# Taking the first of four layer-norm statistics three steps later on VectorE in a batched attention pipeline

## The chip, the cores and the metric

The kernel runs on one core of one Trainium2 chip. The metric is the device time of one execution in microseconds (us); lower is better.

## The reference, cut to what matters

There are 8 batches of 512 tokens with 256 features. Each batch goes through an attention layer whose keys are picked by an argmax, and then all tokens go through a layer of 8 experts of which each token takes 2.

```python
x = x + tanh(g_xattn) * xattn(layernorm(x), ctx)
x = x + tanh(g_ffn) * ffn(layernorm(x))

def xattn(q, kv):                       # per batch; 16 heads of 16
    qp = q @ Wq.T
    scores = qp @ kv.T                  # 512 x 512
    idx = argmax(scores)                # one key row per query
    mk, mv = split(kv[idx] @ Wkv.T)
    attn = softmax(heads(qp) @ mk.T / 4)
    return (attn @ mv) @ Wc.T

def ffn(x):                             # 8 experts, top 2
    top_v, top_i = top_k(x @ gate_w, 2)
    ...                                 # gelu(x @ w1[e] + b1[e]) @ w2[e] + b2[e], weighted
```

Many queries choose the same key, so the kernel keeps each chosen key once, with a count, in at most 192 slots. The softmax then runs over 192 slots and not over 512 keys.

## The kernel before, in words

The program has two large parts. `flow` does everything up to the queues of tokens for the experts; `experts` then runs 39 tiles of 256 tokens through their experts. The change is in `flow`.

`flow` is a software pipeline written out by hand. A generator, `each_step`, goes over periods `p` from -4 to 9 and over 32 steps in each. Every one of the five engines walks through the same (period, step) pairs, and at each step issues the pieces of work that a table of step numbers gives it. An engine carries out its pieces strictly in that order, and waits on semaphores for what other engines or DMAs have yet to deliver. In period `p` these batches are in work:

- batch `p + 4`: its `x` is loaded by SP (step 15, `load_x`, into the single buffer `x_in`), VectorE (DVE) takes one `bn_stats` for each of its four tiles of 128 tokens (`x_stats`, L876, steps in `DVE_X_STATS`) and joins them (`x_moments_of`, step 24). GpSimd (POOL) turns the variance into a factor (L584, step 26) and normalises the four tiles (L592, steps 26 to 29).
- batch `p + 3`: TensorE (PE) transposes the normalised `x` (L1022, step 14) and projects it to queries (L1039, steps 16 and 17).
- batch `p + 2`: PE makes the scores (L1064, steps 5, 7, 9, 11, one tile of queries each), DVE finds each maximum and its index (L808, L809), POOL marks the chosen key (L559). PE counts how often each key is chosen (L1074, step 15); DVE turns that into used or unused (L821, L823, step 17); PE ranks the used keys (L1082, L1083, step 18); DVE makes their positions in the 192 slots (`positions`, step 19, L828 to L838). For batch 0 DVE also writes the 0/1 matrix `place` itself (L836); for the other batches POOL does (L579, step 20). PE then packs keys and values into slots (L1090, L1095, step 22), and ScalarE (ACT) copies them to `k_st` and `v_st` (L673 to L676, step 23).
- batch `p + 1`: PE makes the logits again in query-major form to find each row's maximum (`logits_b`, L1107, one tile a step from step 25 of the period before), and DVE reduces each tile (`take_max`, L849). These tiles and the scores go through a ring of PSUM banks: four banks in negative periods, two from period 0 on. So PE can be at most that many tiles ahead of DVE.
- batch `p`: the softmax and the weighted sum. Batch `p - 1`: output projection, second layer norm, gate and queues.

Periods -4 to -1 fill the pipeline. Within a step, DVE's code comes in this order (much is left out): heads, keys and values, best key, `add`, `x_stats`, `x1_stats`, `used_keys` (17), `positions` (19), `shift_of` (20), `x_moments_of` (24), and last `take_max`. `x_stats` waits for the transfer of `x`:

```python
            def x_stats(b, t):
                dve.wait_ge(x_loaded, 16 * (b + 1))
                chain.step(v.bn_stats(stats[:, 0, t, :], x_in[:, t, :]))
```

and `positions` begins with a wait for the ranks and for all earlier steps of DVE's own chain:

```python
                dve.wait_ge(ranks_ready, s + 1)
                chain.settle()
```

Next to this, 32 pieces of expert weights of 512 KB each are loaded by SP into two staging buffers (L444, L447), rounded by ACT (L770), and their remainder is formed by POOL (L635). SP issues its transfers in program order too.

Of the kernel before, what the change touches and what calls it, by code (L numbers as in the profile page):

```python
# [181 lines left out]
def program(nc, x, ctx_t, g, wq_t, wkv_t, wc_t, gate_w, w1, b1_t, w2, b2, out):  # L182
# [11 lines left out]
    with ExitStack() as whole:  # L194
# [36 lines left out]
        k.dve_steps, k.pool_steps = sem("dve_steps"), sem("pool_steps")  # L231

        flow(nc, k, sem, sb, ps)

        general = Programs(), Programs()
# [5 lines left out]
def flow(nc, k, sem, sb, ps):  # L241
# [6 lines left out]
    with ExitStack() as own:  # L248
# [116 lines left out]

        DVE_HEADS = 13
        DVE_BEST, DVE_KV, DVE_USED, DVE_PLACE = (6, 8, 10, 12), 9, 17, 19
        DVE_X_STATS, DVE_X_MOMENTS = (18, 22, 22, 23), 24
        DVE_ADD, DVE_STATS, DVE_MOMENTS, DVE_SHIFT = (11, 14), (15, 15, 16, 16), 17, 20
        DVE_SPLIT_MAX, DVE_COPY_MAX, DVE_CHOOSE, DVE_SHARES, DVE_QUEUE = 25, 27, 29, 31, 0  # L370

# [2077 lines left out]
```

## Time and profile before

| | |
|---|---|
| median of 3 runs | 993.09 us (992.86 to 994.03) |
| span of the profiled execution (first to last instruction) | 992.7 us |
| filling of the pipeline, periods -4 to -1 | about the first 100 us |
| `flow` up to the end | about 537 us |
| `experts` | the rest, about 456 us |
| TensorE busy | 832.3 us (84%) |
| VectorE busy | 517.9 us (52%) |
| mean granted TensorE clock | 0.914 of full speed |

The profile is of one execution. It gives no time of its own beside its span; the span is 0.4 us under the median of the runs. Busy shares are means over stages with different limits, so each stage has to be read by itself: which engine waits, and for whom. In a timeline, a row is a group of like instructions that follow each other on one engine, with the start, the time from the first start to the last end, and in brackets how long the engine had been idle before it and what ended that.

### The profile page before, as it was taken

Reading aid. Unit: us, or ns where it says so; the run is one execution under the profiler, and the core shown is the slowest. Engines: PE = TensorE matmul, PEld = TensorE weight load, DVE = VectorE, ACT = ScalarE, POOL = GpSimd, SP = SyncE. Lnnn points to the kernel's source line nnn. Section 1 sums busy time; section 2 is a strip of 40 time slices with the busy share of each in tenths; the row PEclk is TensorE's granted clock in tenths of the full one; section 3 lists DMA queues with packets and bytes.
Section 4 is the critical chain, followed back from the end, with each engine's and each line's share of the span. In section 5 each row is a group of like instructions: output and inputs, shape, how many; then the busy total and the mean of one; then the engine's idle time right before and its main releaser. Section 6 shows DMA issues by size and latency. Waiting matters only on the chain. (4 is left out here: it accounts for less than half of the span.)

```text
span 992.7 us, 20863 instructions
## 1 busy us (share of the span) xinstructions
PE 832.3 (84%) x6508; PEld 579.8 (58%) x6509; DVE 517.9 (52%) x1534; ACT 376.7 (38%) x770; POOL 438.1 (44%) x475
## 2 busy tenths in 40 slices
PE   3675899899898989887610899999999999999994
PEld 1243345344343534433310699899989989988984
DVE  3475567766766677762330345444544454454451
ACT  1312263636363544666320333333333433333330
POOL 4766463666566545436541033333433343333334
PEclk9867899989997989898755799999999999999998
DMA  4653424433445261244224122221332233223210
GB/s 160 147 108 107 75 66 90 129 82 108 97 128 98 64 136 49 82 134 138 77 74 165 56 44 46 48 45 33 56 48 41 43 58 48 43 47 49 44 14 1
DMA packets 65691, 76.40 MB, mean 77 GB/s; under 512 B 7392, under 2 KB 59360, under 8 KB 65504
## 3 DMA queue, kind: packets, MB, share of 16 engines
q1 hardware_dynamic: 51328, 58.74, 22.7%
q0 software_dynamic: 14304, 16.93, 9.6%
q8 instruction: 30, 0.49, 0.2%
q14 instruction: 29, 0.24, 0.1%
HBM read 47.68 MB, written 29.53 MB: 78 GB/s over the span
## 5 line engine op out<-in xcount | busy, mean ns | idle before, releaser
L2389 PE MATMUL ps_h<-x_hi,w_split 128*128 128x256 bf16 x1248 | 212.7, 274 | 0.0
L2403 PE MATMUL ps_y<-w_split,hidden 128*128 x1248 | 206.4, 273 | 0.0
L698 ACT ACTIVATE prob<-ps_a 128x512 f32<-128x512 f32 x192 | 113.0, 603 | 181.5 <-PE ps_a L1127 108.2
L2389 PE MATMUL ps_h<-x_lo,w_split 128*128 128x256 bf16 x624 | 171.0, 274 | 0.0
L2403 PE MATMUL ps_y<-w_split,h_lo 128*128 x624 | 170.1, 273 | 0.0
L2299 ACT ACTIVATE hidden<-ps_h,bias 128x256 f32<-128x256 f32 x312 | 131.1, 471 | 88.6 <-PE ps_h L2389 88.6
L849 DVE TENSOR_REDUCE row_max<-ps_d 128x2 f32<-128x384 f32 x237 | 127.9, 551 | 60.8 <-PE ps_d L1107 59.2
L2273 POOL DMA_INDIRECT out<-y,token_at x78 | 131.0, 1680 | 43.8 <-POOL token_at L2271 30.3
L2389 PEld LDWEIGHTS ps_h<-x_hi,w_split 128*128 x1248 | 122.8, 98 | 14.5
L2403 PEld LDWEIGHTS ps_y<-w_split,hidden 128*128 128x128 bf16 x1248 | 122.1, 98 | 14.1
L2269 POOL TENSOR_TENSOR token_f<-tails,ones_f 128x2 f32<-128x2 f32 x39 | 7.8, 200 | 267.5 <-DVE y L2345 266.3
L2342 DVE TENSOR_TENSOR y<-ps_y,b_all 128x512 f32<-128x512 f32 x39 | 27.0, 692 | 174.5 <-PE ps_y L2403 174.5
L1107 PE MATMUL ps_d<-k_st,w_split 96*128 96x192 bf16 x474 | 84.5, 268 | 25.7 <-DVE row_max L849 19.2
L2356 DVE TENSOR_TENSOR h_lo<-hidden 128x512 bf16<-128x512 f32 x156 | 99.7, 686 | 11.3 <-ACT hidden L2299 10.3
L2288 ACT CAST x_hi<-ps_x 128x512 bf16<-128x512 f32 x39 | 22.9, 586 | 213.5 <-PE ps_x L2376 213.5
L635 POOL TENSOR_TENSOR w_split<-w_stage,w_split 128x1024 bf16<-128x1024 f32 x32 | 68.0, 2132 | 63.8 <-ACT w_split L770 63.8
L1107 PEld LDWEIGHTS ps_d<-k_st,w_split 96*128 96x128 bf16 x474 | 40.0, 103 | 77.6 <-DVE row_max L849 32.0
L1144 PE MATMUL ps_o<-prob,v_st 128*32 128x512 f32 x512 | 77.1, 678 | 3.0 <-ACT prob L698 3.0
L611 POOL DMA_INDIRECT queue<-rows,slot x64 | 62.9, 982 | 19.4 <-issue 17.1
L2389 PEld LDWEIGHTS ps_h<-x_lo,w_split 128*128 x624 | 61.4, 98 | 7.4
L2403 PEld LDWEIGHTS ps_y<-w_split,h_lo 128*128 128x128 bf16 x624 | 61.1, 98 | 7.1
L1064 PE MATMUL ps_d<-ctx_sb,q_t 128*128 128x512 f32 x112 | 57.8, 640 | 2.2 <-DVE row_max L849 1.4
(206 smaller groups left out, 1070.8 us busy)
## 6 DMA issues: line engine op xcount, KB each, us to landing
w_stage<-w SPq DMA_DIRECT2D x32, 512.0 KB, 4.1
xg<-queue SPq DMA_DIRECT2D x39, 260.0 KB, 2.8
w_split<-q_split SPq DMA_DIRECT2D x24, 256.0 KB, 7.9
x_in<-x SPq DMA_DIRECT2D x8, 512.0 KB, 3.8
ctx_sb<-ctx_t SPq DMA_DIRECT2D x8, 512.0 KB, 3.6
x<-x SPq DMA_DIRECT2D x8, 512.0 KB, 3.8
q_split<-q_hl SPq DMA_DIRECT2D x16, 256.0 KB, 3.5
out<-x SPq DMA_DIRECT2D x8, 512.0 KB, 5.0
```

Source lines behind the costliest of these rows:

```text
L611: pool.indirect_dma_start(k.queue[:], bass.IndirectOffsetOnAxis(ap=slot[:, t, c:c + 1], axis=0), rows[:, t, :], None).then_inc(scattered, 16)
L635: g.tensor_tensor(lo, stage, hi, ALU.subtract).then_inc(w_lo, 1)
L698: a.activation(prob[n % 2][:, j, :], ps_a[i % 2][:], ACT.Exp, scale=SCALE).then_inc(exp_ready, 1)
L849: v.tensor_reduce(row_max[:, t, 2 * pair:2 * pair + 2], bank[:, 0:2 * SLOTS].rearrange("p (h r) -> p h r", h=2), AX.X, ALU.max).then_inc(m ...
L1064: last = t_.matmul(ps_da[n][:], q_t[:, kt, t * P:(t + 1) * P], ctx_sb[:, kt, :], start=(kt == 0), stop=(kt == KT - 1))
L1107: last = t_.matmul(ps_da[n][:, c * SLOTS:(c + 1) * SLOTS], q_st[m % 3][0:ROW_MAX, 2 * pair + c, t * P:(t + 1) * P], k_st[0:ROW_MAX, m % 3, ...
L1144: last = t_.matmul(ps_o[j * VW:(j + 1) * VW, :], values, probs, start=(key_tile == 0), stop=(key_tile == SLOT_TILES - 1))
L2273: pool.indirect_dma_start(k.out_rows, bass.IndirectOffsetOnAxis(ap=token_at[:, t:t + 1], axis=0), y[s][:, t, :], None, bounds_check=B * L ...
L2299: last = a.activation(hidden[s][:, f, :], ps_h[n][:, c, :], ACT.Gelu, bias=bias[s][:, f:f + 1])
L2356: v.tensor_tensor(h_lo[s][:, both, :], hidden[s][:, both, :], h_hi[s][:, both, :], ALU.subtract).then_inc(h_lo_ready, 1)
L2389: last = t_.matmul(ps_h[n][:, c, :], k.w1_split[:, bass.ds(e, 1), part, kt, f].rearrange("p a f -> p (a f)"), xs[s][:, kt, :], start=(q == ...
L2403: last = t_.matmul(ps_y[s][:, t, :], hs[s][:, f, token], k.w2_split[:, bass.ds(e, 1), part, f, :].rearrange("p a d -> p (a d)"), start=(q ...
```

## The change

One number in a table moves from 18 to 21: the step at which VectorE takes the first of the four `bn_stats` of batch `p + 4`. The other three stay at steps 22, 22 and 23. Nothing is added or removed, and no buffer, transfer or semaphore changes.

```diff
         DVE_HEADS = 13
         DVE_BEST, DVE_KV, DVE_USED, DVE_PLACE = (6, 8, 10, 12), 9, 17, 19
-        DVE_X_STATS, DVE_X_MOMENTS = (18, 22, 22, 23), 24
+        DVE_X_STATS, DVE_X_MOMENTS = (21, 22, 22, 23), 24
         DVE_ADD, DVE_STATS, DVE_MOMENTS, DVE_SHIFT = (11, 14), (15, 15, 16, 16), 17, 20
```

The order of instructions on PE, ACT, POOL and SP is the same before and after. On DVE it differs in six of the eight batches' `x` (2 to 7). The first place is period -2, where no `take_max` work exists yet. These are VectorE's instructions there before; `used`, `unused`, `position` and `chosen` (here the 0/1 matrix of places) belong to batch 0, `stats<-x_in` to batch 2:

```order
L821 TENSOR_SCALAR used<-count 128x4
L823 TENSOR_SCALAR unused<-used 128x4
L878 BN_STATS stats<-x_in 128x6
L828 TENSOR_TENSOR position<-ps_r,unused 128x4
L829 COPY total<-ps_r 128x4
L831 SCALAR_TENSOR_TENSOR offset<-ones_f,total 128x4
L832 TENSOR_TENSOR position<-position,offset 128x4
L836 TENSOR_SCALAR chosen<-column,position 128x192 x4
L838 COPY n_chosen<-offset 128x1
L878 BN_STATS stats<-x_in 128x6 x3
L885 BN_AGGR moments<-stats 128x2 x4
L849 TENSOR_REDUCE row_max<-ps_d 128x2 x2
```

And these are VectorE's instructions at the same place of the changed kernel:

```order
L821 TENSOR_SCALAR used<-count 128x4
L823 TENSOR_SCALAR unused<-used 128x4
L828 TENSOR_TENSOR position<-ps_r,unused 128x4
L829 COPY total<-ps_r 128x4
L831 SCALAR_TENSOR_TENSOR offset<-ones_f,total 128x4
L832 TENSOR_TENSOR position<-position,offset 128x4
L836 TENSOR_SCALAR chosen<-column,position 128x192 x4
L838 COPY n_chosen<-offset 128x1
L878 BN_STATS stats<-x_in 128x6 x4
L885 BN_AGGR moments<-stats 128x2 x4
```

The first statistic, and with it the wait for the transfer of `x`, has gone from ahead of the positions and places to behind them.

The second place stands for the full pipeline (periods 0 to 3). This is the difference on VectorE there, with `row_max` the reduction of one tile of `logits_b`:

```order
 L821 TENSOR_SCALAR used<-count 128x4
 L823 TENSOR_SCALAR unused<-used 128x4
-L849 TENSOR_REDUCE row_max<-ps_d 128x2
-L878 BN_STATS stats<-x_in 128x6
-L849 TENSOR_REDUCE row_max<-ps_d 128x2
+L849 TENSOR_REDUCE row_max<-ps_d 128x2 x2
 L828 TENSOR_TENSOR position<-ps_r,unused 128x4
 L829 COPY total<-ps_r 128x4
```

```order
 L870 RECIPROCAL inverse<-ps_r 128x16
 L871 TENSOR_TENSOR heads<-ps_r,inverse 128x4x4x16
+L878 BN_STATS stats<-x_in 128x6
 L849 TENSOR_REDUCE row_max<-ps_d 128x2
 L878 BN_STATS stats<-x_in 128x6 x2
```

Here the statistic moves from between two reductions, ahead of the positions, to behind the heads of a group, ahead of the reduction of step 21.

## Rows read from the trace of the kernel before

**Rows 1.** The page: busy times by engine, and the last chain by line.
```profile
PE 832.3 (84%) x6508; PEld 579.8 (58%) x6509; DVE 517.9 (52%) x1534; ACT 376.7 (38%) x770; POOL 438.1 (44%) x475
...
PE ps_h L2389 21%; PE ps_y L2403 20%; PE ps_x L2376 2%; DMA xg<-queue 1%; DMA out<-y,token_at 0%; POOL out L2273 0%; DVE y L2342 0%; DVE x_lo L2334 0%; ACT x_hi L2288 0%; DVEq L2230 0%; SPq L2201 0%; SPq L2244 0%; SPq L2240 0%; DVE y L2345 0%; POOL token_f L2269 0%
```

**Rows 2.** Waits from 43 to 56 us: total, times, longest.
```profile
DVE stats L878 <- DMA x_in<-x: 11.0, 1, 11.0
...
PE ps_e L1090 <- DVE chosen L836: 9.5, 1, 9.5
...
POOL variance L584 <- DVE moments L885: 4.7, 1, 4.7
```

**Rows 3.** Timeline of VectorE, period -2: start, us, what, count.
```profile
39.69 0.17 DVE L823 TENSOR_SCALAR unused<-used 128x4 f32<-128x4 bf16 x1
50.84 0.43 DVE L878 BATCH_NORM_STATS2 stats<-x_in 128x6 f32<-128x256 f32 x1 [10.98 <-DMA x_in<-x]
...
51.84 0.16 DVE L832 TENSOR_TENSOR position<-position,offset 128x4 f32<-128x4 f32 x1
52.04 0.81 DVE L836 TENSOR_SCALAR chosen<-column,position 128x192 bf16<-128x192 f16 x4
...
52.83 1.07 DVE L878 BATCH_NORM_STATS2 stats<-x_in 128x6 f32<-128x256 f32 x3
54.00 0.38 DVE L885 BATCH_NORM_AGGREGATE moments<-stats 128x2 f32<-128x6 f32 x4
56.23 1.02 DVE L849 TENSOR_REDUCE row_max<-ps_d 128x2 f32<-128x384 f32 x2 [1.85 <-PE ps_d L1107]
```

**Rows 4.** Timeline of TensorE, periods -2 and -1.
```profile
43.21 0.17 PE L1083 MATMUL ps_r<-used,ones_bf 128*128 128x4 bf16 x1
52.90 0.87 PE L1090 MATMUL ps_e<-chosen,key_cols 128*98 128x192 bf16 x4 [9.53 <-DVE chosen L836]
53.57 1.18 PE L1095 MATMUL ps_e<-value_cols,chosen 128*128 128x17 bf16 x24
55.71 0.80 PE L1107 MATMUL ps_d<-k_st,w_split 96*128 96x192 bf16 x4 [0.95 <-issue]
...
61.11 3.75 PE L1064 MATMUL ps_d<-ctx_sb,q_t 128*128 128x512 f32 x4
...
65.86 1.91 PE L1064 MATMUL ps_d<-ctx_sb,q_t 128*128 128x512 f32 x4
```

**Rows 5.** Timeline of ScalarE, period -2.
```profile
45.37 1.04 ACT L667 CAST q_hl<-q_t 128x1024 bf16<-128x1024 f32 x1
54.79 0.51 ACT L673 ACTIVATE k_st<-ps_e,key_add,key_mul 98x192 bf16<-98x192 f32 x1 [8.38 <-PE ps_e L1095]
```

**Rows 6.** Timeline of SP's DMA issues: the load of batch 2's x.
```profile
42.33 0.50 SPq L452 DMA_DIRECT2D x_in<-x  x1
```

**Rows 7.** Timeline of GpSimd, period -1.
```profile
62.82 2.12 POOL L635 TENSOR_TENSOR w_split<-w_stage,w_split 128x1024 bf16<-128x1024 f32 x1
66.47 0.19 POOL L558 CAST best<-top_at 128x1 f32<-128x1 uint32 x1 [1.53 <-DVE top_at L809]
...
69.38 0.19 POOL L558 CAST best<-top_at 128x1 f32<-128x1 uint32 x1 [1.03 <-DVE top_at L809]
```

**Rows 8.** Timeline of VectorE in period 0, around steps 18 and 23.
```profile
130.03 0.42 DVE L878 BATCH_NORM_STATS2 stats<-x_in 128x6 f32<-128x256 f32 x1
132.85 0.56 DVE L849 TENSOR_REDUCE row_max<-ps_d 128x2 f32<-128x384 f32 x1 [2.40 <-PE ps_d L1107]
...
138.61 0.56 DVE L849 TENSOR_REDUCE row_max<-ps_d 128x2 f32<-128x384 f32 x1 [0.86 <-PE ps_d L1107]
```

**Rows 9.** Windows: length, busy us (count) of PE, PEld, DVE, ACT, POOL; PEclk, DMA share, GB/s.
```profile
56.00:61.00 5.00, 5.00 (x26) 2.05 (x23) 4.78 (x11) 1.62 (x2) 5.00 (x4) 0.50 0.00 0
61.00:65.00 4.00, 3.95 (x7) 1.48 (x6) 1.46 (x4) 0.00 (x0) 3.94 (x3) 0.50 0.91 209
65.50:68.00 2.50, 2.50 (x23) 1.25 (x12) 1.98 (x6) 1.21 (x2) 1.42 (x2) 1.00 1.14 116
```

## The prediction

> **What bounds the kernel now.** I read the page first. TensorE is busy 84% of the span and the last chain holds only lines of the expert part [rows 1], so that part is bound by TensorE matmuls in a fixed order and the change can't touch it; it will start earlier or later by what `flow` gains or loses. The chain ends there and says nothing on `flow`, so I went through the waits, stage by stage, around every place where the order of VectorE changes. In the full pipeline these waits are a few tenths of a microsecond. In period -2 they are large: VectorE waits 11.0 us for the transfer of batch 2's `x`, and in the same stretch TensorE waits 9.5 us for VectorE's places of batch 0 [rows 2]. The timelines show that these are one wait. VectorE is done with `unused` at 39.86, then stands until 50.84 in front of the first `bn_stats`, and only behind it come positions and places, done at 52.85 [rows 3]. TensorE had the ranks ready at 43.38, packs from 52.90, and starts `logits_b` at 55.71 [rows 4]. So the reader should see a queue: positions need nothing but the ranks, yet they stand behind an instruction that needs a DMA issued only at 42.33 [rows 6].
>
> **The change at period -2.** It takes the waiting instruction out of the way of the positions. Step by step:
>
> *Places.* From the end of the first statistic (50.84 + 0.43 = 51.27) to the end of the places (52.04 + 0.81 = 52.85) it is 1.58 us [rows 3]. They can start when the ranks are there, 43.38: places at 43.38 + 1.6 = 45.0.
>
> *Pack.* 52.90 to 53.57 + 1.18 = 54.75 is 1.85 us [rows 4]: done at 46.85. ACT's copy of the packed keys stands behind the rounding of the queries, which ends at 45.37 + 1.04 = 46.41 [rows 5], so it is free. From its start (54.79) to the first `logits_b` (55.71) it is 0.92 us [rows 4, 5]: `logits_b` starts near 47.8, 7.9 us earlier.
>
> *What is late next.* VectorE must reduce those tiles, and its reductions stand behind all four statistics of batch 2. Nothing in the chain of that transfer is moved: SP issues it at 42.33 as before [rows 6], so I keep the landing at 50.84. Four statistics take 0.43 + 1.07 = 1.5 us, the gap to the moments is 54.00 - 53.90 = 0.1, the moments take 0.38 [rows 3]: the first `row_max` can start at 50.84 + 2.0 = 52.8. By then TensorE has filled the four banks. Before, it started at 56.23, and it had waited 1.85 us for TensorE [rows 3]. The gain here is 56.23 - 52.8 = 3.4 us. The other 4.5 us of TensorE's head start are lost to the transfer, which still bounds the stage.
>
> *Does the shift live on?* From 56.23 to the scores of batch 1 at 61.11 VectorE is busy 4.78 of 5 us [rows 9], with TensorE held by the bank ring, so the scores start when the reductions free a bank: they move with VectorE, to about 57.7. Two engines move by less. The moments end at 52.8 in place of 54.38, so POOL's variance comes only 1.6 us earlier; before, it waited 4.7 us for them [rows 2, 3]. POOL's last piece before the chosen keys ends at 64.94, then at 63.3; the first index, which it awaited for 1.53 us until 66.47, comes at 63.1. That costs 0.2 us at that one instruction, and the next has a wait of 1.03 us to take it back [rows 7]. SP's next weight piece hangs on the same POOL work and also moves by 1.6 us only, and so the query loads behind it; these are needed a period later. So I let the full 3.4 us pass into period -1 and from there on, since every later piece hangs on a semaphore and not on a fixed time.
>
> **The change in period -1 and in the full pipeline.** The four statistics cost the same; one moves. In period 0 the first one stood at 130.03, and the reduction behind it then waited 2.40 us for TensorE until 132.85 [rows 8]. It was hidden in that idle time, so the positions behind the reduction gain nothing. At its new place it comes between busy instructions and delays the reductions of steps 21 and 22 and the last statistic by 0.42 us. The next reduction, at 138.61, has waited 0.86 us for TensorE [rows 8]: it takes the delay in, and 0.44 us stay. TensorE's ring of two banks needs the reduction of step 21 only at step 23. Four periods have this pattern; price 0, and if that cover were gone 4 x 0.42 = 1.7 us. The nearest row gives cover, so I take 0.
>
> **The clock.** TensorE's granted clock is 0.50 (1.2 GHz) from 56 to 65 us although TensorE is busy 5.00 of 5 us with bf16 `logits_b` from 56 to 61; it is 1.00 (2.4 GHz) from 65.5, after some 4 us of float32 scores. The first tile of scores takes 3.75 us at the low level, a later one 1.91 at the high one [rows 4, 9]. I take the rise at the same instruction as before, so the price of the clock is 0, between -1.84 (the first tile of scores is already fast) and +1.84 for each further tile that stays slow.
>
> The Trainium skill, "TensorE: Matmul & The Clock Gate", Part 1, says that the idle state is the throttled one and that sustained matmul activity releases it. By that rule the earlier pack and `logits_b` would make the clock rise before the first scores, and the sum would be 1.84 us lower. The trace does not agree in that stretch: 5 us of unbroken `logits_b` did not raise it.
>
> **The sum.** -3.4 + 0 + 0 = -3.4 us. From the span 992.7 that is 989.3; the median lies 0.4 above the span, so 989.7 us, 0.34% less.
>
> **The rivals.**
>
> 1. *The clock rises sooner.* TensorE works from about 45 to 49 and again from 52.8, and no longer lies idle for 9.5 us in one piece. If that lifts the clock before the first scores, -3.4 - 1.84: 987.8 us. For it: two bursts and less idle time. Against it: rows 9, where dense `logits_b` did not do it.
>
> 2. *Part of the gain is absorbed.* Either the side that moves by 1.6 us (POOL, SP, the query loads) turns out to be last somewhere in period -1, or the 0.42 us show in each of four full periods. Both leave some 1.7 us: 991.4 us. Against it: POOL's wait of 1.53 us, and the 0.86 us of cover in VectorE [rows 7, 8].
>
> 3. *Nothing comes of it.* The transfer of `x` still holds batch 2, and a later wait in the filling of the pipeline (another transfer, the weights) ends when it did: 993.1 us. For it: the 7.9 us on TensorE shrink to 3.4 at once. Against it: all loads are issued in reply to work that moves too.
>
> 4. *Slower: the clock stays low for longer.* The place is the four tiles of scores in period -1, with `logits_b` now paced by VectorE and more often idle before them. If all four ran at 1.2 GHz, the price is 4 x 1.84 = 7.4, less the 3.4 gained: +4.0, 997.1 us. From the third slow tile on (5.5 - 3.4 = +2.1) it decides. Against it: float32 scores raised the clock before within the first tile.
>
> **How the numbers follow.** Two tenths of a percent is 2.0 us, about what a measurement of this kernel can tell from no change. Chances: my forecast 0.68 (own range 989.0 to 990.4), rival 1 0.09, rival 2 0.13, rival 3 0.06, rival 4 0.04. Faster takes the forecast, rival 1 and the better edge of rival 2: 0.79. The rest of rival 2 and rival 3 are no change: 0.17. Slower 0.04. The range reaches from rival 1 to rival 2, 987.8 to 991.4, with about half of each beyond it or at its edge.
>
> **What the profile would show.** Right: VectorE's places end near 45.0 and its wait for the transfer of `x`, until about 50.8, follows them; the pack starts near 45.0; `logits_b` starts near 47.8; the first `row_max` near 52.8; the first scores of batch 1 near 57.7, still 3.75 us long; from then on every row of period 0 stands 3.4 us earlier, with an idle time of some 2.8 us ahead of the reduction of step 18 and of some 0.4 us ahead of that of step 23. Wrong: the transfer landing later than 50.84 moves the gain down one for one; a wait of TensorE longer than before in period -1 for the chosen keys or the places, written by POOL, is rival 2; scores at another length are rivals 1 or 4.

## The result and the profile after

The changed kernel took 988.11 us (median of 5 runs, 986.64 to 988.61) against 992.86 us before on the same chip (991.54 to 994.03). The ratio is 0.9946 with a 95% interval of 0.9930 to 0.9963: 5.4 us less, or 3.7 to 7.0 us. (The two medians by themselves lie 4.75 us apart; the interval belongs to the ratio.) The span of the profiled execution went from 992.7 to 986.8 us. The forecast was 3.4 us less. Its sign and its place were right; its size lies just below that interval.

VectorE in period -2 after the change, the rows that answer to [rows 3] (timeline: start, us, what, count, idle before):

```profile
42.59 0.16 DVE L828 TENSOR_TENSOR position<-ps_r,unused 128x4 f32<-128x4 f32 x1 [4.78 <-PE ps_r L1083]
...
43.26 0.81 DVE L836 TENSOR_SCALAR chosen<-column,position 128x192 bf16<-128x192 f16 x4
...
47.54 1.41 DVE L878 BATCH_NORM_STATS2 stats<-x_in 128x6 f32<-128x256 f32 x4 [3.41 <-DMA x_in<-x]
49.05 0.38 DVE L885 BATCH_NORM_AGGREGATE moments<-stats 128x2 f32<-128x6 f32 x4
49.34 0.99 DVE L849 TENSOR_REDUCE row_max<-ps_d 128x2 f32<-128x384 f32 x2
```

The positions now wait only for the ranks (4.78 us, until 42.54), the places end at 44.07, and the wait for `x` stands behind them. The first reduction starts 1.80 us behind the landing of `x` (49.34 - 47.54). Before, it was 5.39 us (56.23 - 50.84, [rows 3]).

TensorE at the same place, the rows that answer to [rows 4]:

```profile
44.12 0.53 PE L1090 MATMUL ps_e<-chosen,key_cols 128*98 128x192 bf16 x4 [1.58 <-DVE chosen L836]
...
46.43 0.80 PE L1107 MATMUL ps_d<-k_st,w_split 96*128 96x192 bf16 x4 [0.95 <-issue]
47.02 0.85 PE L1107 MATMUL ps_a<-k_st,w_split 96*128 96x192 bf16 x4
49.93 0.97 PE L1107 MATMUL ps_d<-k_st,w_split 96*128 96x192 bf16 x4 [2.06 <-DVE row_max L849]
...
54.19 3.75 PE L1064 MATMUL ps_d<-ctx_sb,q_t 128*128 128x512 f32 x4
```

The 9.53 us of idle time ahead of the pack are 1.58 us. TensorE fills four banks (two rows of four matmuls, two to a tile), then stands for 2.06 us until VectorE has reduced one. The first scores come at 54.19, 6.92 us earlier than at 61.11, and still take 3.75 us.

What differs beside that is upstream of the change. SP's issue of the same `x`, the row that answers to [rows 6]:

```profile
40.35 0.50 SPq L452 DMA_DIRECT2D x_in<-x  x1
```

It is 1.98 us earlier than in the profile before, and the landing is 3.30 us earlier (47.54 against 50.84), so the transfer also took 1.3 us less. Yet no instruction ahead of that point has changed its place. The difference in the first reduction splits without rest: 56.23 - 49.34 = 6.89 = 3.30 (landing) + 3.59 (5.39 - 1.80, what lies between landing and reduction). Whether the 3.30 are chance or belong to the change was the open question.

Period 0, the rows that answer to [rows 8]:

```profile
126.31 0.56 DVE L849 TENSOR_REDUCE row_max<-ps_d 128x2 f32<-128x384 f32 x1 [2.74 <-PE ps_d L1107]
...
129.20 0.43 DVE L878 BATCH_NORM_STATS2 stats<-x_in 128x6 f32<-128x256 f32 x1
...
132.07 0.56 DVE L849 TENSOR_REDUCE row_max<-ps_d 128x2 f32<-128x384 f32 x1 [0.53 <-PE ps_d L1107]
```

The statistic left an idle time that grew from 2.40 to 2.74 us, and took 0.33 of the 0.86 us of cover ahead of the reduction of step 23. Both reductions stand 6.54 us earlier than before: nothing is gained or lost between them.

### The profile page after: what moved, and what is told of

Same layout as the page of the kernel before. It is cut to its first block and busy times, and to the rows that moved or that the text cites. A ratio compares the mean times of both kernels' runs of the same rounds, so it can differ in the third digit from the quotient of the medians.

```text
span 986.8 us, 20863 instructions
## 1 busy us (share of the span) xinstructions
PE 834.3 (85%) x6508; PEld 580.4 (59%) x6509; DVE 518.1 (53%) x1534; ACT 376.8 (38%) x770; POOL 438.5 (44%) x475
## 5 line engine op out<-in xcount | busy, mean ns | idle before, releaser
L635 POOL TENSOR_TENSOR w_split<-w_stage,w_split 128x1024 bf16<-128x1024 f32 x32 | 68.1, 2134 | 64.6 <-ACT w_split L770 64.5
```

Of the source, the lines that this page charges most:

```text
L635: g.tensor_tensor(lo, stage, hi, ALU.subtract).then_inc(w_lo, 1)
```

## The experiments

Theory A: the change takes the 3.6 us between the landing of `x` and the first reduction, and the landing itself moves by chance. Its rivals were B (the earlier landing comes from the change), C (the other five places give a part), D (something else bounds the filling of the pipeline) and later E and F. All ratios are to runs of the kernel before on the same chip, each with a 95% interval.

### The kernel before once more, and the changed kernel once more

No edit.

> The kernel before once more, to see how far two profiles and two sets of times of one program lie apart. Theory A (the change is worth the 3.6 us that lie between the landing of x and the first reduction in the two profiles, 5.39 against 1.80 us, and the other 3.3 us between the two profiles are chance: an earlier landing of the first transfers and of x): ratio 1.000 within 0.1%, and in its profile a landing of x that differs from 50.84 us by one us or more, with the first reduction again 5.4 us behind it. Theory B (the landing of x is earlier because of the change): a landing of x at 50.8 within 0.5 us here.

Measured: ratio 0.9998 (0.9985 to 1.0010), span 990.4 us. In its profile `x` landed at 47.23 us, not at 50.84:

```profile
47.23 0.43 DVE L878 BATCH_NORM_STATS2 stats<-x_in 128x6 f32<-128x256 f32 x1 [9.12 <-DMA x_in<-x]
...
48.02 0.87 DVE L831 TENSOR_TENSOR_SCAN offset<-ones_f,total 128x4 f32<-128x4 f32 x1
...
53.31 1.02 DVE L849 TENSOR_REDUCE row_max<-ps_d 128x2 f32<-128x384 f32 x2 [1.85 <-PE ps_d L1107]
```

So the unchanged program lands `x` 3.6 us apart in two executions, earlier even than the changed one did. The reduction is 6.08 us behind the landing; 0.7 of that is the scan at L831, which took 0.87 in place of 0.17 us (more on that in the last section).

> The changed kernel once more. Theory A: the first reduction again 1.8 to 2.0 us behind the landing of x, the landing itself somewhere between 47 and 51 us; faster by 3.6 us, a ratio of 0.9964. Theory B: landing near 47.5 us again and a ratio near 0.9946, 5.4 us.

Measured: 0.9953 (0.9936 to 0.9969), span 987.2 us. This time `x` landed at 49.92 us, and the reduction again followed 1.80 us behind:

```profile
49.92 1.40 DVE L878 BATCH_NORM_STATS2 stats<-x_in 128x6 f32<-128x256 f32 x4 [7.28 <-DMA x_in<-x]
51.43 0.38 DVE L885 BATCH_NORM_AGGREGATE moments<-stats 128x2 f32<-128x6 f32 x4
51.72 0.99 DVE L849 TENSOR_REDUCE row_max<-ps_d 128x2 f32<-128x384 f32 x2
```

In the four profiles of the old order with no transfer moved (before, once more, all but batch 2, third time) `x` landed at 49.4 us in the mean, in the four of the changed order at 49.2. The single early landing was chance, and theory B falls. The ratio, 4.7 us, lies between the two expectations and its interval holds both.

### Only batch 2, and all but batch 2

```diff
-                for t in due(p + 4, DVE_X_STATS, step):
+                for t in due(p + 4, (21, 22, 22, 23) if p == -2 else DVE_X_STATS, step):
```

This is on the kernel before; the other one has `(18, 22, 22, 23) if p == -2` on the changed kernel.

> Only batch 2's first statistic (period -2) is taken at step 21; all others stay at step 18. Theory A: all of the gain is there, so this is as fast as the changed kernel, within 0.1%. Rival C (a part of the gain comes from the five other places, each worth up to 0.42 us): 1 to 2 us slower than the changed kernel.

> Batch 2's first statistic stays at step 18, ahead of the positions; all others go to step 21. Theory A: no change to the kernel before, within 0.1%, with VectorE again waiting for x ahead of the positions. Rival C: 1 to 2 us faster than before.

Measured: only batch 2, 0.9958 (0.9942 to 0.9974); all but batch 2, 1.0000 (0.9988 to 1.0012). The first had `x` at 50.21 and the reduction at 52.02 (1.81 behind), the second `x` at 49.18 and the reduction at 54.55 (5.37 behind). The gain is in period -2, and the five other places are worth nothing that these runs can tell from zero (1.2 us at most). Rival C falls.

### Batch 2's x loaded first, in both orders

```diff
-                if step == SP_X and p > -4 and is_batch(p + 4):
+                if step == (6 if p == -2 else SP_X) and p > -4 and is_batch(p + 4):
```

> The changed kernel, with batch 2's x loaded ahead of the two weight pieces and the context that SP issued before it in period -2. Theory A (in the changed kernel the transfer of x bounds the first reduction, which comes 1.8 us behind its landing): x lands near 44.5 us in place of 47.5 to 50.2, the first reduction then comes right behind the first logits_b, near 47.5, in place of 49.3 to 52.0; some 3.5 us faster than the changed kernel, ratio to before 0.992 to 0.993. Rival D (another transfer or POOL bounds period -1, and the landing is not what counts): ratio 0.995 to 0.996, as the changed kernel.

> The kernel before (first statistic at step 18, ahead of the positions) with the same earlier load of x. Theory A: the first reduction stays 5.4 us behind the landing as long as x lands after the ranks; x lands near 44.5, the first reduction comes near 50, in place of 53.3 to 56.2; ratio 0.995 to 0.996. What the order of the statistic is worth shrinks to 2 to 3 us (this kernel against the one with both). Rival D: ratio 1.000.

Measured: 0.9932 (0.9912 to 0.9952) with the changed order, 0.9932 (0.9913 to 0.9951) with the old one. Both are faster than either kernel, and in these runs the order of the statistic is then worth nothing. The old order with `x` first shows why:

```profile
43.82 0.43 DVE L878 BATCH_NORM_STATS2 stats<-x_in 128x6 f32<-128x256 f32 x1 [3.40 <-DMA x_in<-x]
45.34 0.16 DVE L828 TENSOR_TENSOR position<-ps_r,unused 128x4 f32<-128x4 f32 x1 [1.09 <-PE ps_r L1083]
...
49.40 1.02 DVE L849 TENSOR_REDUCE row_max<-ps_d 128x2 f32<-128x384 f32 x2 [1.06 <-PE ps_d L1107]
```

`x` lands 1.5 us ahead of the ranks, so the statistic fits into the wait for them and holds up nobody. The first reduction (49.40; 49.37 with the changed order) waits for `logits_b` in both. The expectation had the two 2 to 3 us apart, because it let `x` land behind the ranks. In these executions the ranks came at 45.3, and the old order costs something only if the landing is later than the ranks. In the eight profiles of the original and the changed order without a moved transfer, the ranks were ready between 41.05 and 44.2 us, so there an `x` that lands at 43.8 could still find the ranks waiting. What the order is worth with `x` first and early ranks was not measured. Why the ranks were late is the subject of a later experiment.

### SP doesn't hold its queue for the query stack

This edit stands on the changed order with `x` first.

```diff
                 sp.wait_ge(q_stored, 32 * (s + 1))
+                if s:
+                    sp.wait_ge(q_loaded, 48 * s)
...
-                sp.wait_ge(q_loaded, 48 * (s + 1))
```

> As the changed kernel with x first, and SP no longer waits for the landing of a batch's query stack right after its issue, but ahead of the next stack. So x of batch 2 is issued near 36.5 us, when TensorE has turned batch 1, and the weight pieces some 2 us earlier. Theory A: x lands before the ranks and bounds nothing any more; the first reduction is bound by logits_b, as with x first alone, so at most 1 us better than that: ratio 0.991 to 0.993. Rival D (weights bound the filling): another 2 us or more, 0.990 or less.

Measured: 0.9929 (0.9911 to 0.9948), as with `x` first alone. SP issued `x` at 36.10 us and the two weight pieces at 37.05 and 39.17, and nothing came of it: the first reduction waited for `logits_b` until 49.87. Once `x` no longer bounds the stage, the ranks do; weight pieces issued earlier than in the run before brought nothing.

### The statistics behind three reductions

On the changed kernel, all four statistics and the moments go to step 28 in period -2.

```diff
-                for t in due(p + 4, DVE_X_STATS, step):
+                for t in due(p + 4, (28,) * 4 if p == -2 else DVE_X_STATS, step):
...
-                if step == DVE_X_MOMENTS and is_batch(p + 4):
+                if step == (28 if p == -2 else DVE_X_MOMENTS) and is_batch(p + 4):
```

> The changed kernel with all four statistics and the moments of batch 2 in step 28, so three reductions (steps 25 to 27) stand ahead of the wait for x. Theory A: TensorE has filled four banks by then, so VectorE does three reductions (3 x 0.47 = 1.4 us) while it waits, and the first scores come 1.4 us earlier than in the changed kernel: ratio 0.9940 to 0.9950. Rival D: no difference to the changed kernel. If POOL's normalising of batch 2, which then starts no earlier, bounded period -1, it would be no faster either.

Measured: 0.9953 (0.9936 to 0.9970), as the changed kernel. In this execution the places came late, near 48.6, so three reductions could start only at 51.19 and `x` was there when they were done:

```profile
51.19 1.02 DVE L849 TENSOR_REDUCE row_max<-ps_d 128x2 f32<-128x384 f32 x2 [2.53 <-PE ps_d L1107]
52.12 0.55 DVE L849 TENSOR_REDUCE row_max<-ps_a 128x2 f32<-128x384 f32 x1
52.59 1.39 DVE L878 BATCH_NORM_STATS2 stats<-x_in 128x6 f32<-128x256 f32 x4
```

VectorE never waited for `x` here, so there was no such wait to fill, and the profile doesn't tell the theories apart. It shows only that this order brings nothing on the mean of the runs.

### GpSimd's weight remainders out of the way

The ranks were late in the last four kernels because TensorE's count of the chosen keys waited 3.28 us for VectorE, where it had been 1.24 us before. The rows are from the kernel with `x` first and the changed order. TensorE's count, then VectorE:

```profile
38.87 0.58 PE L1074 MATMUL ps_r<-ones_bf,chosen 128*128 128x1 bf16 x16 [3.28 <-DVE chosen L813]
```

```profile
34.28 2.41 DVE L813 TENSOR_SCALAR chosen<-column,best 128x512 bf16<-128x512 f16 x1
...
38.32 0.49 DVE L813 TENSOR_SCALAR chosen<-column,best 128x512 bf16<-128x512 f16 x1
```

And GpSimd in the same stretch:

```profile
33.23 1.22 POOL L592 TENSOR_SCALAR x_in<-x_in,moments,rstd 128x256 f32<-128x256 f32 x1
34.41 4.25 POOL L635 TENSOR_TENSOR w_split<-w_stage,w_split 128x1024 bf16<-128x1024 f32 x2
```

The marking of this key, 0.35 us in the kernel before, took 2.41 us and ended at 36.69, just behind the end of GpSimd's first remainder (34.41 + 2.13 = 36.54). To test this, the remainders of pieces 0 and 1 go to step 18 of period -2, behind the values, once with `x` first and once without, both in the changed order.

```diff
-                for i in pieces(p, step, 1):
+                for i in ([0, 1] if step == 18 else [] if step < 18 else pieces(p, step, 1)) if p == -2 else pieces(p, step, 1):
```

> The changed kernel with x of batch 2 first in SP's row, and with GpSimd's remainders of weight pieces 0 and 1 moved from steps 5 and 11 of period -2 to step 18, behind the values. Theory E (VectorE's marking of a chosen key took 2.41 us in place of 0.35 in the profile of the kernel with x first, since GpSimd's remainder ran at the same time; the 1.1 us of 'used' are the same thing): both instructions take 0.5 us or less, the ranks come 1 to 2 us sooner; ratio 0.990 to 0.992. Rival: the durations stay, and the ratio is 0.993 as with x first alone.

Measured: 0.9933 (0.9916 to 0.9949). The durations are as theory E has them: all markings between 30 and 38 us took 0.35 or 0.36 us, and `used` took 0.17 us:

```profile
36.77 0.35 DVE L813 TENSOR_SCALAR chosen<-column,best 128x512 bf16<-128x512 f16 x1
...
37.99 0.17 DVE L821 TENSOR_SCALAR used<-count 128x4 bf16<-128x4 f32 x1
```

But the time did not follow. The places were done at 44.6 and the pack at 45.9, and then ScalarE, whose weight piece was now loaded later (issued at 43.57 in place of 41.44 us), stood in front of the packed keys:

```profile
46.82 1.04 ACT L770 CAST w_split<-w_stage 128x1024 bf16<-128x1024 f32 x1 [3.39 <-DMA w_stage<-w]
47.77 1.04 ACT L667 CAST q_hl<-q_t 128x1024 bf16<-128x1024 f32 x1
48.72 0.50 ACT L673 ACTIVATE k_st<-ps_e,key_add,key_mul 98x192 bf16<-98x192 f32 x1
```

A wait for a weight piece had taken the place of the stall, by the same pattern as the wait this study is about: an instruction that needs a transfer, in front of one that needs nothing but TensorE.

> The changed kernel with GpSimd's remainders of weight pieces 0 and 1 at step 18 of period -2, and x where it was, behind two weight pieces and the context. Theory A: the weight pieces wait for those remainders, and x behind them is issued some 1 to 2 us later than 41 us; the first reduction stays 1.8 us behind the landing, so what the shorter VectorE instructions bring is lost: ratio 0.995 to 0.997. If the ranks and not x bounded the changed kernel, it would be 1 to 2 us faster than it, 0.993.

Measured: 0.9961 (0.9947 to 0.9975), within the range of theory A. `x` was issued at 43.70, landed at 50.67, and the first reduction came at 52.47: again 1.80 us behind.

### A late x, in both orders

```diff
-                if step == SP_X and p > -4 and is_batch(p + 4):
+                if step == (22 if p == -2 else SP_X) and p > -4 and is_batch(p + 4):
```

> The kernel before, with the load of batch 2's x moved from step 15 to step 22 of period -2, behind the next weight piece. Theory A: x is issued near 48 and lands near 52 us, 3 us later than before; positions, pack and logits_b follow it, the first reduction is 5.4 us behind the landing, near 57.5: 3 us slower than before, ratio 1.003. Rival F (the gain of the change is not set by the order but by when the clock and GpSimd's work fall): no such one for one.

> The changed kernel with the same late load of x. Theory A: the landing bounds this one as well, one for one, with the first reduction 1.8 us behind it, near 54: ratio near 0.9995, and 3.6 us faster than the kernel before with the same late load. If the real gain of the change in order is larger, as the first times said (5.4 us), the two differ by 5 us.

Measured: old order 1.0028 (1.0015 to 1.0041), changed order 0.9992 (0.9976 to 1.0008). They are 0.0036 or 3.6 us apart, as expected. The loads were issued and landed later than expected, and not alike: 49.80 and 54.35 us in the profile of the old order, 47.97 and 52.46 in the other. So these two profiles, with spans 5.3 us apart, hold 1.9 us of difference in landing. The old order:

```profile
54.35 0.43 DVE L878 BATCH_NORM_STATS2 stats<-x_in 128x6 f32<-128x256 f32 x1 [13.86 <-DMA x_in<-x]
...
59.74 1.02 DVE L849 TENSOR_REDUCE row_max<-ps_d 128x2 f32<-128x384 f32 x2 [1.85 <-PE ps_d L1107]
```

And the changed order:

```profile
52.46 1.41 DVE L878 BATCH_NORM_STATS2 stats<-x_in 128x6 f32<-128x256 f32 x4 [7.07 <-DMA x_in<-x]
...
54.27 0.99 DVE L849 TENSOR_REDUCE row_max<-ps_d 128x2 f32<-128x384 f32 x2
```

5.39 us behind the landing in the one, 1.81 in the other: the reduction follows the landing one for one at the distance of its order, which rival F had denied. The times agree only roughly, since a profile is one execution: the old order was 2.8 us slower than the kernel before, with a landing 3.5 us later than the latest of its profiles.

### The plain pair again, and the pair without GpSimd's remainders

The edit of the first two is that of the section on the remainders, on the old and on the changed order; the last two have none.

> The kernel before with GpSimd's remainders of pieces 0 and 1 at step 18 of period -2, the old order of the statistic. Theory A: first reduction 5.4 us behind the landing; 3.6 us slower than the same kernel with the changed order. If the surplus over 3.6 us in the first comparisons comes from GpSimd's subtractions, which hold VectorE in the old order more than in the new, it is gone here, and the two differ by 3.6 us within 1 us.

> The changed kernel with those remainders at step 18, once more, on the same chip as its counterpart with the old order. Theory A: first reduction 1.8 us behind the landing, 3.6 us faster than the counterpart.

> The kernel before a third time, as the base of the pair. Ratio 1.000 within 0.1%.

> The changed kernel a third time. If the gain is 3.6 us and the surplus of the first times was chance, the ratio is 0.9964 within 0.001. If there is a true surplus of 1 us, it is 0.9954 or less, as in the first two sets.

Measured, all on one chip: with the remainders late, 1.0014 (1.0001 to 1.0027) in the old order and 0.9969 (0.9956 to 0.9981) in the changed one, 0.0045 or 4.5 us apart. The plain pair: 0.9991 (0.9978 to 1.0003) and 0.9963 (0.9949 to 0.9977). The changed kernel gains 3.7 us against all runs of the kernel before there, 2.8 us against the copy beside it. So the surplus of the first times was not repeated by the plain pair. With GpSimd's work moved the difference is 4.5 us, within the 1 us around 3.6 that was expected, and no smaller than in the plain pair: that GpSimd's subtractions make a surplus is not shown.

In each profile in which VectorE waited for an `x` that landed behind the ranks, the first reduction stands at one of two distances; the one exception, 6.08 us, holds the scan that took 0.7 us longer:

| kernel | landing of x | first reduction | between |
|---|---|---|---|
| before | 50.84 | 56.23 | 5.39 |
| before, once more | 47.23 | 53.31 | 6.08 |
| all but batch 2 | 49.18 | 54.55 | 5.37 |
| before, late x | 54.35 | 59.74 | 5.39 |
| before, remainders late | 49.62 | 55.00 | 5.38 |
| before, third time | 50.34 | 55.72 | 5.38 |
| changed | 47.54 | 49.34 | 1.80 |
| changed, once more | 49.92 | 51.72 | 1.80 |
| only batch 2 | 50.21 | 52.02 | 1.81 |
| changed, remainders late | 50.67 | 52.47 | 1.80 |
| changed, late x | 52.46 | 54.27 | 1.81 |
| changed, remainders late, again | 50.93 | 52.74 | 1.81 |
| changed, third time | 49.11 | 50.91 | 1.80 |

## Why the prediction was off in size

**The mechanism was right.** The first statistic, waiting for its transfer, held the positions; the changed order runs them when the ranks are there; the pack, `logits_b` and the filled banks follow; and the landing of `x` is what bounds the stage next. Doing only batch 2 gives the gain, all but batch 2 gives none that shows.

**The term of 3.4 us was a little small.** It put the first reduction 2.0 us behind the landing; it is 1.8, since the four statistics in a row take 1.41 us and not 1.5, and the first reduction starts 0.29 us after the start of the moments and not after their 0.38. So 3.6 us, which is what the two orders with a late `x` differ by.

**The step that failed is "so I keep the landing at 50.84".** The reason given, that nothing in the chain of that transfer is moved, was true, but one profile doesn't tell when it lands. In the profiles in which no transfer was moved (before and changed, each three times, only batch 2, all but batch 2) it landed between 47.23 and 50.84, and the profile on which the forecast rested had the latest of them. The two profiled spans, 5.9 us apart, hold 3.3 us of that luck, and the forecast time of 989.7 us started from an execution that landed `x` 1.4 us later than the mean of the old order. The landing doesn't explain a larger gain in the mean of many runs, since it came at 49.2 us in the changed order and at 49.4 in the old. What set the first five runs on each side 5.4 us apart in place of 3.6 is not known.

**How much is the gain, then?** Six comparisons differ in the order alone and have `x` behind the ranks: 5.4 us (3.7 to 7.0), 4.7, 4.2 (only batch 2), 3.6 (both with a late `x`), 4.5 (both with the remainders late) and 3.7 us. Each of the later ones holds 3.6 us within its uncertainty of 1.4 to 2 us; the first one, with 5 runs on each side, is the outlier. The mean of the six is 4.4 us. By the medians of the runs alone the six are 4.75, 4.4, 3.7, 3.8, 4.1 and 3.4 us, 4.0 in the mean. The profiles show 3.6 us of it, by the two distances. They also show small extras in some executions: the scan held for 0.7 us once in the old order, and a first tile of scores of 3.46 to 3.69 us in five of the seven profiles of the new order in the table above, because the clock rose before its end; in the old order it is 3.75 in five of six, and 3.66 in one. That is 0.1 us in the mean. At the last instruction the profiles show no surplus: it stands 940.8 us behind the landing in the mean of the six old ones and 937.9 in the mean of the seven new ones, 2.9 us apart, with single ones up to 2.4 us off their mean. Whether the mean gain holds up to 1 us more than 3.6 stays open.

**The shift of 3.4 us was let pass to the end**, through POOL and SP that move by less. For the filling of the pipeline that was right: POOL lost a little at its first chosen key and took it back. From the first scores of batch 1 (-6.92) to the moments of batch 4 (-6.55) only 0.4 us are lost. Behind that, this pair of profiles loses another 1.2: the first transpose of the expert part stands at 543.69 in place of 549.01, 5.32 us earlier. The stretch from the first reduction to that transpose took 490.1 to 494.4 us over the profiles of the table, in both orders, so a loss of this size can't be told from chance.

**The price of 0 in the full pipeline was right**, with the cover as read: 2.74 us of idle time (some 2.8 forecast) and 0.53 (0.4). (The prediction also says that all waits in the full pipeline are a few tenths; its own [rows 8] has one of 2.40 us.)

**Rival 1, an earlier rise of the clock**, did not happen in the form given. TensorE's granted clock was 0.50 (1.2 GHz) from 50 to 54 us, with TensorE busy all of the time, and through the first tile of scores in the changed kernel too (54.19, 3.75 us), though TensorE had lain idle for 1.58 and 2.06 us in place of 9.53. The Trainium skill's rule that sustained activity releases the throttle ("TensorE: Matmul & The Clock Gate", Part 1) again didn't show for `logits_b`. What it would have added, 1.84 us, would by chance have given about the measured 5.4 us: a reader with the times alone would have taken the wrong rival for shown. The row of 3.75 us decides. A small piece of the rival is real, the 0.1 us in the mean named above. Against rival 4 the prediction said that the clock had risen within the first tile before; the rows say otherwise. It was 0.50 from 64.6 to 65.0 us, past the end of that tile (61.11 + 3.75 = 64.86), and 0.89 in the mean from 65.0 to 65.5.

**Rivals 2, 3 and 4** were not seen. The ranges of the gain leave no room for rivals 3 and 4, and no wait was found in the filling that absorbs half of it.

## What to carry to other kernels

In a program written out by hand, look for an instruction that waits for a transfer and stands in front of one whose inputs are ready. Its price is at most the time by which the landing is later than those inputs. Here the places came 7.9 us too late (52.85 against 45.0), of which the end saw 3.6, since the same transfer bounded the next instruction too; once the load was issued early enough to land before the ranks it was nothing. Loading `x` first was worth more (0.9932) than moving the statistic (0.9946 to 0.9963), and where both were measured the two didn't add.

When a term hangs on the moment at which a transfer lands, read it from several executions, or take the difference between two fixed distances to it (5.39 and 1.80 us here), which stayed within 0.02 us in twelve of thirteen profiles while the landing moved by 7.

## What was not expected of the hardware

**VectorE's instruction held by GpSimd's.** Three kinds of small VectorE instruction took far longer when GpSimd ran a subtraction, and ended with it. In the kernel before, `used` (L821), 0.17 us elsewhere, took 1.15 us:

```profile
38.51 1.15 DVE L821 TENSOR_SCALAR used<-count 128x4 bf16<-128x4 f32 x1
```

and GpSimd's remainders ended 0.03 us before it:

```profile
35.29 4.34 POOL L635 TENSOR_TENSOR w_split<-w_stage,w_split 128x1024 bf16<-128x1024 f32 x2
```

The scan of the kernel before once more (48.02 to 48.89) ended with GpSimd's `q_hl` (46.75 + 2.12 = 48.87), and the marking of 2.41 us as shown above. With the remainders moved, the marking and `used` went back to 0.35 and 0.17 us, so this is shown by an experiment and not only by the times agreeing. The scan shows it once more: in the changed order the moved remainders end at 43.26, 43.30 and 43.55 us, and the scan behind the ranks, started shortly before, took 0.37 to 0.44 us and ended at 43.28, 43.33 and 43.57. The Trainium skill has it on the page "SBUF — State Buffer", section "SBUF: two separate sides": VectorE and GpSimd share a pair of ports, which GpSimd and certain kinds of VectorE instruction need, and one of them holds it for a whole instruction while the other is blocked. The rows agree in the ends. The page also says that whoever starts first gets the pair; here the marking starts at 34.28 in the records, ahead of the subtraction at 34.41 but while GpSimd's preceding instruction (33.23 to 34.45) still ran, and it was held until the subtraction's end. The starts in the records don't decide who waits, as the next rows show.

**Which instruction is held differs between profiles.** In the kernel before, the same marking started at 35.15, also 0.14 us ahead of GpSimd's subtraction, and took 0.35 us; there `used` was held. Of the 14 profiles that had the remainders at the old place, eight are like that, with `used` at 1.12 to 1.17 us. In the other six the marking took 2.40 or 2.41 us and `used` 0.17: in the two kernels with `x` first, the one without SP's hold, the one with the statistics at step 28, and the two with a late `x`. In the last three, nothing ahead of that place differs from the kernel before, so the edits are not the reason. But all six were taken on one chip, in two sets of runs, and six of the eight others on two other chips (for the first pair the chip is not on record). Whether it goes with the chip or falls by chance in each execution can't be told from these runs. The instruction itself loses 2.06 us, and `used` gives 1 us of it back: from the start of the marking to the end of `unused` it is 5.79 us (34.28 to 40.07, `x` first, changed order) in place of 4.71 (35.15 to 39.86, before). The difference may be a part of the kernel's spread (988.6 to 995.5 us for the kernel before over all sets of runs); how much was not measured.
